# A gated attention block and a mixture of experts: the filter rows move into the convolution's block, and the last head and the beginning of the FFN are put in another order

## The reference, cut to what matters

```python
# x, ctx: (16, 512, 1024); 64 heads of 8 rows each; L = 1024
def xattn(k, v, q, ssm_kernel, D):           # k = v = ctx, q = layernorm(x)
    kv = einsum('bhil,bhjl->bijhl', k_, v_)  # products of the 8 rows of a head
    y = irfft(rfft(kv, n=2*L) * rfft(ssm_kernel, n=2*L))[..., :L]   # causal convolution along L
    out = einsum('bijhl,bhil->bjhl', y + kv * D, q_)
x = x + tanh(g_xattn) * xattn(...)
z = layernorm(x)
def ffn(z):                                  # 8192 tokens of width 1024, F = 512
    shared = (x1 * silu(x2)) @ shared_w2     # x1, x2 = halves of z @ shared_w1
    aff = sigmoid(z @ gate_w + expert_bias)  # 7 experts, top 2 of each token
    # each expert keeps its best 1170 tokens (capacity), works them with its own w1, w2,
    # and adds the weighted result to those tokens
x = x + tanh(g_ffn) * ffn(z)
```

## Time and profile before

| | before |
|---|---|
| median of three runs | 4221.51 us |
| the profiled execution's own time | 4221.36 us |
| its span, first to last instruction | 4219.6 us |
| PE (TensorE matmul) busy | 4113.0 us, 97% |
| DVE (VectorE) busy | 2500.4 us, 59% |
| ACT (ScalarE) busy | 1955.9 us, 46% |
| POOL (GpSimd) busy | 1240.4 us, 29% |

### The profile page before, as it was taken

How to read it: one execution, slowest core, us unless ns; L and a number is a source line. 1 busy time by engine, 2 the same in 40 slices (tenths; PEclk the granted TensorE clock), 3 DMA queues, 4 the chain that set the end, 5 groups by cost and what they waited for, 6 DMA issues and landing times.

```text
span 4219.6 us, 71650 instructions
## 1 busy us (share of the span) xinstructions
PE 4113.0 (97%) x25930; PEld 3755.9 (89%) x25930; DVE 2500.4 (59%) x2916; ACT 1955.9 (46%) x2581; POOL 1240.4 (29%) x1264
## 2 busy tenths in 40 slices
PE   6999999999999999997999999999999999999997
PEld 6999999999999999996788788888898888988986
DVE  6999999999999999995434432222323323323331
ACT  6888888888888888873111111111212212212120
POOL 1444444444444444430000034540011111111111
PEclk9999999999999999998999999999999999999999
DMA  7889888888888988896232324234334433443332
GB/s 179 217 216 222 216 226 218 216 221 218 223 220 216 223 217 220 221 228 108 80 114 66 120 72 128 88 93 114 104 95 115 100 79 96 103 95 96 86 92 46
DMA packets 280369, 634.08 MB, mean 150 GB/s; under 512 B 45840, under 2 KB 111866, under 8 KB 280246
## 3 DMA queue, kind: packets, MB, share of 16 engines
q1 hardware_dynamic: 218582, 413.89, 32.0%
q0 software_dynamic: 61664, 218.41, 28.4%
HBM read 311.03 MB, written 170.16 MB: 114 GB/s over the span
## 4 chain that ended last, share of the span: by engine, by line
PE 48%; DMA 2%; DVE 2%; issue 1%; ACT 0%; SPq 0%; POOL 0%; DVEq 0%; ACTq 0%; POOLq 0%
PE mem_acc L1844 11%; PE mem_acc L1845 11%; PE mem_acc L1846 11%; PE moe_ps L1862 5%; PE moe_ps L1864 5%; PE moe_ps L1863 5%; PE moe_psT L1834 1%; DMA out<-moe_y,moe_add_i 1%; DMA moe_y<-out 1%; DMA out<-moe_y 1%; DVE moe_zl L1744 1%; ACT moe_zh L1518 0%; DVE moe_hid L1757 0%; DVE moe_y L1771 0%; DMA moe_zin<-zT_d 0%
## 5 line engine op out<-in xcount | busy, mean ns | idle before, releaser
L1844 PE MATMUL mem_acc<-moe_zh,moe_w1h 128*128 128x512 f32 (+2 forms) x2336 | 848.3, 363 | 22.5 <-issue 16.9
L1845 PE MATMUL mem_acc<-moe_zl,moe_w1h 128*128 128x512 f32 (+2 forms) x2336 | 846.5, 362 | 0.0
L1846 PE MATMUL mem_acc<-moe_zh,moe_w1l 128*128 128x512 f32 (+2 forms) x2336 | 843.9, 361 | 0.0
L878 PE MATMUL mem_acc<-att_kv_hi,att_tz_hi 128*128 128x288 f32 x2560 | 766.5, 299 | 40.3 <-DMA att_kv_lo<-att_kv 40.3
L879 PE MATMUL mem_acc<-att_kv_lo,att_tz_hi 128*128 128x288 f32 x2560 | 754.6, 295 | 0.0
L880 PE MATMUL mem_acc<-att_kv_hi,att_tz_lo 128*128 128x288 f32 x2560 | 754.6, 295 | 0.0
L1757 DVE TENSOR_TENSOR moe_hid<-mem_acc,moe_act_s 128x512 f32<-128x512 f32 (+2 forms) x148 | 91.7, 620 | 876.1 <-PE mem_acc L1846 839.6
L878 PEld LDWEIGHTS mem_acc<-att_kv_hi,att_tz_hi 128*128 128x128 f32 x2560 | 481.1, 188 | 52.0 <-issue 40.3
L1844 PEld LDWEIGHTS mem_acc<-moe_zh,moe_w1h 128*128 128x128 f32 x2336 | 440.0, 188 | 73.6 <-issue 23.5
L1846 PEld LDWEIGHTS mem_acc<-moe_zh,moe_w1l 128*128 128x128 f32 x2336 | 441.7, 189 | 50.0
L1845 PEld LDWEIGHTS mem_acc<-moe_zl,moe_w1h 128*128 128x128 f32 x2336 | 440.5, 189 | 49.7 <-issue 0.2
(11 more groups left out here) (205 smaller groups left out, 8108.8 us busy)
## 6 DMA issues: line engine op xcount, KB each, us to landing
att_kv_lo<-att_kv POOLq DMA_DIRECT2D x128, 1152.0 KB, 9.7
att_kT<-in_cT SPq DMA_DIRECT2D x64, 512.0 KB, 6.4
att_xn<-in_x SPq DMA_DIRECT2D x64, 512.0 KB, 8.3
out<-att_x SPq DMA_DIRECT2D x64, 512.0 KB, 7.2
z_d<-att_z SPq DMA_DIRECT2D x64, 512.0 KB, 5.9
zT_d<-att_zT SPq DMA_DIRECT2D x64, 512.0 KB, 8.6
moe_zin<-zT_d SPq DMA_DIRECT2D x64, 512.0 KB, 7.0
moe_y<-out SPq DMA_DIRECT2D x128, 256.0 KB
```

The costliest lines, as they stand in the source:

```text
L878: nc.tensor.matmul(acc, w_hi[:, cols], x_hi, start=start, stop=False, skip_group_check=True)
L1844: nc.tensor.matmul(acc, w1h[j][:, c, b, :], zh[:, c, 0:w], start=(c == 0), stop=False)
L1845: nc.tensor.matmul(acc, w1h[j][:, c, b, :], zl[:, c, 0:w], start=False, stop=False)
L1846: last = nc.tensor.matmul(acc, w1l[j][:, c, b, :], zh[:, c, 0:w], start=False, stop=(c == C - 1))
```

## The change: the filter rows, the last head, and the first two groups

**Filter rows.** The first block is gone; its work is done in the convolution's block (VectorE, lines 815 to 832; SyncE, 306, 307 and 366 to 372). The keys of head 0 are now the first load. The filter tiles lie over `prod` and `y1`. The Toeplitz loads of head 0 wait for all four stores (`filters_out`, 64). The low parts of head 0 are computed by VectorE (`first_low`), no longer by `minus_high` and `add_low`; the counts of later heads are lower by one.

**Four places for z.** In group 0, z tiles 2 and 3 go to the upper half of `raw` (`first_z`), in group 1 to the lower half (`next_z`). In exchange the second piece of w1 (j = 1) is loaded after all four z tiles are split, and w2 is loaded after those of group 1 are.

**Last head.** ScalarE's and VectorE's steps for z and w1 stand at other places; the last `turn_o` goes to another PSUM bank (`psQ`); `center` of the last head moves from GpSimd to VectorE; a dummy Silu stands at the end of the block on ScalarE.

**Scores.** `make_scores` runs on VectorE after the second of the four pieces of group 0, no longer after the whole group and the z tiles of group 1.

```diff
@@ conv_stage, sync @@
+            sp.dma_start(kT[:, :, :, :].rearrange("p t b i -> p (t b i)"), cT[0]).then_inc(kT_in, 16)
+            sp.dma_start(full[:, P - 1:P - 1 + L], ssm_kernel).then_inc(loaded, 16)
+            sp.dma_start(d_col[:, 0:1], D.rearrange("(h a) -> h a", a=1)).then_inc(loaded, 16)
...
             def load_ffn_z(t):
                 sp.wait_ge(y_done, NT * (H - 1))
-                wait(sp, ffn_zh_set, t - 1)
-                wait(sp, ffn_zl_set, t - 1)
-                sp.dma_start(mem.zin[t % 2][:, :], zT_d[t].rearrange("p c n -> p (c n)")).then_inc(ffn_z_in[t % 2], 16)
+                if t >= 2:
+                    sp.wait_ge(multiplied, 2 * (H - 1))
+                    sp.wait_ge(u_hi_set, H)
+                    sp.wait_ge(u_lo_set, H)
+                sp.dma_start(mem.first_z[t], zT_d[t].rearrange("p c n -> p (c n)")).then_inc(ffn_z_in[t], 16)
             def load_ffn_w1(j):
                 if j == 1:
-                    sp.wait_ge(multiplied, 2 * (H - 1))
-                    sp.wait_ge(u_hi_set, H)
-                    sp.wait_ge(u_lo_set, H)
+                    sp.wait_ge(ffn_zh_set, GT)
+                    sp.wait_ge(ffn_zl_set, GT)
...
-            load_keys(0)
+            sp.wait_ge(rounded, 2)
+            sp.dma_start(filt_hi, f_hi[:, :].bitcast(F32)).then_inc(filters_out, 16)
+            sp.wait_ge(split, 2)
+            sp.dma_start(filt_lo, f_lo[:, :].bitcast(F32)).then_inc(filters_out, 16)
+            sp.wait_ge(zeroed, 1)
+            sp.dma_start(z_d[T:T + P, :], zero[:, :]).then_inc(filters_out, 16)
+            sp.dma_start(out[T:T + P, :], zero[:, :]).then_inc(filters_out, 16)
             load_x(0, 0)
+            load_keys(1)
+            sp.wait_ge(filters_out, 64)
             load_filter(0, 0)
-            load_keys(1)
             load_sums(0)
@@ conv_stage, vector @@
+            def first_low(half):
+                dve.wait_ge(hi_set, half + 1)
+                nc.vector.tensor_tensor(kv_lo[0][:, keys_of(half)].rearrange("p t b i -> p (t b i)"),
+                                        kv[half][:, :, :, :].rearrange("p t b i -> p (t b i)"),
+                                        kv_hi[0][:, keys_of(half)].rearrange("p t b i -> p (t b i)").bitcast(F32),
+                                        ALU.subtract).then_inc(first_low_set, 1)
...
             residual(H - 1, 1, 0)
+            ffn_w1_low(1, 1)
             residual(H - 1, 1, 1)
-            ffn_w1_low(1, 1)
+            dve.wait_ge(x1_set, 2 * H)
+            dve.wait_ge(rooted[1], ROOT * (H - 1))
+            nc.vector.tensor_scalar(minus_mean[:, :], sums[:, 0:1], sums[:, 1:2], -1.0 / L,
+                                    ALU.add, ALU.mult).then_inc(centered, 1)
@@ conv_stage, scalar @@
             ffn_w1_high(3, 0)
+            nc.scalar.activation(square[:, :], minus_mean[:, :], ACT.Silu)
@@ conv_stage, tensor: turn_o @@
-                wait(pe, x1_set, 2 * h + half)
+                apart = isinstance(h, int) and h == H - 1 and half == 1
+                if apart:
+                    pe.wait_ge(q_set, 4 * H)
+                else:
+                    wait(pe, x1_set, 2 * h + half)
+                bank = psQ if apart else psO
@@ experts, sync @@
+            sp.dma_start(logit, logit_d).then_inc(logit_in, 16)
+            sp.dma_start(g[:, :], g_ffn.rearrange("(a e) -> a e", a=1).to_broadcast([P, 1])).then_inc(const, 16)
             load_z(1, 0)
             load_z(1, 1)
-            sp.dma_start(logit, logit_d).then_inc(logit_in, 16)
-            sp.dma_start(g[:, :], g_ffn.rearrange("(a e) -> a e", a=1).to_broadcast([P, 1])).then_inc(const, 16)
+            for t in (2, 3):
+                sp.dma_start(mem.next_z[t], zT_d[GT + t].rearrange("p c n -> p (c n)")).then_inc(next_z_in[t - 2], 16)
             sp.wait_ge(list_made, 4)
...
-            load_w2(0, shared_w2[0])
-            load_z(1, 2)
-            load_z(1, 3)
             sp.wait_ge(rdone, SCORE_STEPS)
...
+            sp.wait_ge(zh_set, 2 * GT)
+            sp.wait_ge(zl_set, 2 * GT)
+            load_w2(0, shared_w2[0])
             load_z(2, 0)
             load_z(2, 1)
@@ experts, vector: group @@
+                    elif j == 1:
+                        for step in places:
+                            route(step)
+                        dve.wait_ge(gate, 1)
```

More of the change, by code:

```diff
@@ L208, in conv_stage @@
     with ExitStack() as ctx:
+        with ExitStack() as first:
+            m = Pool(nc, first, "fil")
+            full = m.sb("full", [H, FROM + SUMS])
+            both = m.sb("both", [H, SUMS])
+            f_hi = m.sb("hi", [H, PAD], F32R)
+            f_lo = m.sb("lo", [H, PAD], F32R)
+            d_col = m.sb("d", [H, HD])
+            zero = m.sb("zero", [P, L])
         m = Pool(nc, ctx, "att")
+        prod = m.sb("prod", [P, M, HD * HD])
+        y1 = m.sb("y1", [P, G, B, PAIRS])
+        assert FROM + 2 * SUMS + 2 * PAD + HD + L <= M * HD * HD + G * B * PAIRS
         old = mem.conv
@@ L250, in conv_stage @@
         psL = m.ps("psL", [P, BANK])
+        first_low_set = m.sem("first_low_set")
+        cleared, loaded, tapped, summed, rounded, split, zeroed, filters_out = (
+            m.sem(n) for n in ("cleared", "loaded", "tapped", "summed", "rounded", "split", "zeroed", "filters_out"))
         const = m.sem("const")
@@ L301, in wait, with wait_low @@
                 eng.wait_ge(sem, value)
+        def wait_low(eng, h, half):
+            if isinstance(h, int) and h == 0:
+                eng.wait_ge(first_low_set, half + 1)
+            else:
+                wait(eng, lo_in[half], 16 * h)
         def steady(eng, step):
@@ L513, in squares @@
                 act.wait_ge(kx_set, 2 * h + 2)
-                wait(act, lo_in[half], 16 * h)
+                wait_low(act, h - 1, half)
                 if half == 0:
@@ L628, in _ @@
             high(0, 0, 0)
[L629 removed]
             high(0, 0, 1)
[L631 removed]
+            act.sem_inc(minus_set, 2)
+            act.wait_ge(const, 48)
+            nc.scalar.activation(tg[:, :], g[:, :], ACT.Tanh).then_inc(gate, 1)
             high_u(0)
@@ L634, in _ @@
             keys_on(1)
+            act.wait_ge(filters_out, 64)
             def step(h, u, ahead, back, back2):
@@ L684, in step @@
                     keys(h + 2)
-                if not ahead:
-                    ffn_z_high(3)
                 conv_out(h, 6)
@@ L780, in residual @@
                     wait(dve, centered, h)
-                nc.vector.scalar_tensor_tensor(out=x1[:, cols], in0=psO[:, :], scalar=tg[:, 0:1], in1=xn[u][:, cols],
+                turned = psQ if isinstance(h, int) and h == H - 1 and half == 1 else psO
+                nc.vector.scalar_tensor_tensor(out=x1[:, cols], in0=turned[:, :], scalar=tg[:, 0:1], in1=xn[u][:, cols],
                                                op0=ALU.mult, op1=ALU.add,
@@ L791, in pairs @@
                 dve.wait_ge(kx_set, 2 * h + 2)
-                wait(dve, lo_in[half], 16 * h)
+                wait_low(dve, h - 1, half)
                 tiles = keys_of(half).start // G
@@ L846, in step @@
                 if not ahead:
+                    ffn_z_low(2)
+                multiply(h, u, 0)
+                if not ahead:
+                    ffn_z_low(3)
                     ffn_w1_low(0, 0)
-                    ffn_z_low(2)
-                    ffn_z_low(3)
-                multiply(h, u, 0)
                 if back2:
@@ L1806, in group @@
                         result(prev, t, half)
-                if prev is None:
-                    for step in places:
-                        route(step)
-                    dve.wait_ge(gate, 1)
                 if turning:
```

137 lines of the change are left out of this document (61 added, 76 removed).

## The result

The changed kernel takes 4188.51 us (median of 4 runs, 4186.12 to 4190.57) against 4225.91 us for the kernel before in the same series (4219.62 to 4230.53): ratio 0.9917, 95% interval 0.9905 to 0.9929. So it is 0.8% faster, 37.4 us by the medians. A later series gave 0.9916 (0.9899 to 0.9932). The profiled run took 4186.12 us with a span of 4184.2, 35.4 us less than the span before. Forecast: 4179, range 4171 to 4193. The kernel before is 4.4 us slower here than in the three runs from which the forecast set out, so the saving of 37.4 is the fairer number to lay beside its 42.3.

What follows compares the result with a forecast made beforehand. TensorE (PE) bounds the kernel, busy 97% of the span, so only its 106.6 us of waits and low-clock stretches can shrink. Span 4219.6 less 17.8 + 8.7 + 1.3 + 9.4 + 5.1 = 42.3, plus 1.8, gives 4179.1 us; range 4171 to 4193.

Steps and rivals of the forecast that it cites:

- the likeliest case: Whole kernel: the forecast's terms come, time 4179 us, own bounds 4172 to 4186; chance 0.70.
- The start: Wait ahead of the first matmul: two parallel chains, DMA the later, bring it from 40.3 to 22.5 us; 17.8 less.
- Rival 1: At the start: zero stores, x and keys crowd the DMA queue, first matmul at 30, time 4187; chance 0.11.
- The last head: End of the attention loop: reordered steps remove TensorE's waits and keep its clock up; 8.7 us less.
- Rival 2: In the last head: w1's second piece lands late, PE waits 3.4 us, clock's 2.6 lost, time 4185; chance 0.07.
- The change of blocks: At the new block's start: the dummy Silu takes ScalarE's table load off the path; 1.3 of 5.6 us less.
- Between the groups: Between the FFN's first two groups: four z tiles already lie there, so PE starts at 1983.2, not 1992.6; 9.4 us less.
- Scores and w2: FFN group 1, first tally: scores moved to group 0, wait 2.6 instead of 5.56, clock kept; 5.1 us less.
- The clock term: Behind the first tally in group 1: a 2.6 us wait should not drop TensorE's clock; 2.1 us less.
- S + 10: 10 us after PE's start in group 1; PE feels w2's landing only beyond that, expected at 8 to 10.
- Rival 3: In group 1: w2 lands 24.2 us after PE's start, the tally waits 16.8 us, time 4195; chance 0.05.
- Rivals 4 and 5: 4: VectorE slower in the loop on moved buffers, 4284, chance 0.02; 5: start stays held, only FFN terms come, 4197, 0.03.

Runs made afterwards that it cites:

- The square: Changed kernel against three variants: without the dummy Silu, with TensorE's identity wait moved to group 1, and with both; 4192.16, 4195.52 and 4195.71 us.

## Why the prediction was right, and where it was not

The stretches that it named are the ones that got shorter, and four of its five terms came for their greater part by the mechanism named. Its own bounds for the likeliest case, 4172 to 4186, were too narrow: 4188.51 lies 2.5 above them, and inside the range only because that was widened for rivals, none of which came in full.

**The start, 17.8 against 15.75.** The mechanism held: VectorE's low part was ready at 17.4 (forecast 17.0), the DMA chain was the later one, and its last transfer ended the wait. It was mis-sized in three places: the filter's chain began 0.6 us later, because its D row landed at 6.57; the store to `out` took 6.4 us where I counted 5.8; and the loads' issue and landing took 6.3 where I had 5.5. Rival 1, a crowded queue, was the same fault at its full size; a quarter of its 7.5 us came. Whether the x and the keys ahead of the loads delay them by their place in the ring or by sharing was not settled: with the keys and the stores behind them instead, the loads landed no faster (6.7 us against 5.9).

**The last head, 8.7 against 9.28.** Right in its steps: no wait for `oT` or x1, the second piece right behind the gates, full clock. Undoing either order brought back its wait, 2.50 and 1.50 us. Rival 2 did not come, though the third piece of w1 had no cover, as forecast: ScalarE waited 2.46 us for its load, and in seven of the other profiles TensorE waited 0.2 to 0.6 us for `att_zT` behind it.

**The change of blocks, 1.3 against 0.07.** The step that failed. I put the table load on the path because it stood right ahead of the silu; beside it, ending at nearly the same time, stood GpSimd's identity by way of a wait of TensorE's sequencer. The trace of the kernel before had it, in GpSimd's rows:

```profile
1949.87 0.29 POOL L48 TENSOR_SCALAR_AFFINE_SELECT moe_ident<-moe_ident 128x128 f32<-128x128 f32 x1
```

The identity was ready at 1950.16, and the table load ended at 1950.32; from the identity to the silu it is 0.13 us in the changed kernel, so the silu could have come only 0.05 us sooner without the load. The gap shrank by 0.05, from 5.57 to 5.52. The square shows both prices by TensorE's gap: 0.3 us for the load under that wait, 1.3 without it.

**Between the groups, 9.4 against 8.86.** Right: four tiles back to back, and TensorE starts 0.1 us behind the last low part (1956.21 + 2.35). The gap itself shrank by 9.43, from 16.59 to 7.16; the rest is group 0, which ran 0.57 us longer: at its start thirteen matmuls ran at the low clock in place of ten, 0.43 us apart and not 0.23.

**Scores and w2, 5.1 against 3.06.** The wait fell by 2.66 where I had 3.0. The clock term is the mis-sized one: I argued that 2.6 us of wait would not drop the clock, since 3.36 had not yet done so in the last head, and counted 2.1. It dropped after 2.90, and only 0.4 came. The row was true for the moment only: the four transposes ran at the full clock, but one us later, in the same stretch of the kernel before, the clock was down:

```profile
1928.00:1929.00 1.00, 0.96 (x20) 0.52 (x18) 0.57 (x1) 0.00 (x0) 0.00 (x0) 1.00 0.00 0
1929.00:1930.00 1.00, 0.00 (x0) 0.00 (x0) 1.00 (x3) 0.28 (x1) 0.62 (x1) 0.56 0.00 0
```

w2 landed at 10.6, just past the S + 10 from which I said TensorE feels it. Rival 3, a landing of 24.2 us, did not come. The move of the scores also is what lets w2 be asked for at group 1's start: undone alone, it costs 18.4 us at the silu behind the tally, which no term of mine held.

**Behind, 0 against -1.6**, in waits for the residual and between them, within what such profiles differ by.

Rivals 4 and 5 did not come: TensorE is busy 1790.00 us of the loop's window, as before, and the start has its gain. Of the distance to the median, 9.5 us, these terms explain 6.9; 2.4 is that the profiled run was the fastest of its four.

## What to carry to other kernels

- When a wait is removed, ask what else was due in the same stretch, on sequencers as well: of two conditions that end within 0.1 us of each other either one alone is worth little (here 0.3 and 0.0 us of gap), and both together 1.3. A square of four kernels shows it.
- A wait on TensorE of a few us can cost its clock too. Shortening it from 5.56 to 2.72 us did not give that part back; taking it away did. Here one short piece of VectorE's program moved ahead of 3.5 us of other work did both.
- Follow a moved block of work through every queue that waits for it: the scores' price was set by a load that stood behind a load that waited for them.

## What the hardware showed unexpectedly

- The granted clock fell behind waits of 2.72, 2.90 and 3.29 us and behind two of 1.83 and 0.67 close together, and did not behind one of 1.50. Behind one of 3.36 it held for about one us more and then fell.
- Two writes of 64 KB in small packets (16,742 packets under 512 B in the 50 us around them, nearly all theirs) kept the DMA engines busy to about 1957 us, and SyncE 14.36 us on one issue. The residual loads behind them took 7.2 us to land and not 4.4, and w2 behind those 10.6 and not 8.7; over all profiles with the writes ahead w2 took 10.0 to 13.9.
- The adding DMA of 1152 KB took 13.7 and 17.4 us at the start where the loop's median is 9.7.
